# A two-layer decoder in six stages: stage boundaries reordered, weight splits halved and paced, and the second attention's order of work changed

## The reference, cut to what matters

```python
x = x + L0_attn(layernorm(x))     # stage A: latent attention
x = x + L0_xattn(layernorm(x), ctx, ctx, 0, mask)   # stage B, "second attention"
x = x + L0_ffn(layernorm(x))      # stage C: x @ W_up.T + LoRA of the expert with the largest gate
x = x + L1_attn(layernorm(x))     # stage D: gated FFN (1248) and a six-term series
x = x + L1_xattn(layernorm(x), ctx)                 # stage E: 8 "heads" of 64, 128 keys
x = x + L1_ffn(layernorm(x))      # stage F: relu(x @ up)**2 @ down and a routed latent part, then layernorm
...
# stage B, per sequence: 32 heads of 16, keys and values shared by 4 heads
scores = einsum('bgrst,..', xq, xk) / 4 + mask
out = einsum('bgrst,btgd->bsgrd', softmax(scores), xv)
# stage D
dterm = exp(log|delta| * m - discount[m-1])         # m = 1 .. 6, delta = x @ gate_w.T - local_point
out = approx_up @ approx_out.T + sum((dterm * approx_up) @ fuse[m-1].T) \
      + (silu(x @ ffn_gate_w.T) * (x @ ffn_up_w.T)) @ ffn_down_w.T
```

## Time and profile before

| what | value |
|---|---|
| median of 3 runs | 1254.52 us (1254.37 to 1260.95) |
| the profiled execution's own time | 1251.37 us |
| its span | 1249.6 us, mean granted PE clock 0.955 |
| PE busy | 1109.9 us (89%) |
| DVE busy | 738.6 us (59%) |
| ACT busy | 464.2 us (37%) |
| POOL busy | 423.4 us (34%) |

### The profile page before, as it was taken

One profiled execution on the slowest core, in us unless ns is written; L12 is line 12 of the kernel. 1 busy time (PEld: TensorE's weight loads), 2 busy tenths in 40 slices (PEclk: granted clock), 3 DMA queues, 4 the chain that ended last, 5 costly groups with the idle time before them and its releaser, 6 DMA issues.

```text
span 1249.6 us, 23652 instructions
## 1 busy us (share of the span) xinstructions
PE 1109.9 (89%) x9380; PEld 594.0 (48%) x9380; DVE 738.6 (59%) x1255; ACT 464.2 (37%) x813; POOL 423.4 (34%) x365
## 2 busy tenths in 40 slices
PE   6798886988898789998799999999888799999992
PEld 3454453666664344444344444444455444444441
DVE  6777774788887674348613511532479833646456
ACT  4566562555555534321111211211256522223220
POOL 2355495788851320039500000000043300506053
PEclk9897995899999999999999999999999999999997
DMA  6000100111110111222100000000000000000000
GB/s 231 2 3 2 29 2 27 40 41 41 39 55 24 62 42 44 99 78 76 51 1 1 0 0 0 1 1 1 3 11 7 1 1 1 26 8 34 0 34 34
DMA packets 29011, 35.91 MB, mean 29 GB/s; under 512 B 5882, under 2 KB 20499, under 8 KB 28788
## 3 DMA queue, kind: packets, MB, share of 16 engines
q1 hardware_dynamic: 27506, 34.53, 8.4%
q10 hardware_dynamic: 1410, 0.06, 0.1%
HBM read 30.24 MB, written 4.19 MB: 28 GB/s over the span
## 4 chain that ended last, share of the span: by engine, by line
PE 58%; DVE 19%; issue 3%; ACT 3%; POOL 0%; DVEq 0%; ACTq 0%; POOLq 0%
PE p_up L116 10%; PE p_up L118 9%; PE p_up L117 9%; PE p_y L116 7%; PE p_y L118 7%; PE p_y L117 7%; DVE b_top L1355 2%; DVE wf_lo L241 2%; DVE e_den L2197 1%; PE p_y L1511 1%; ACT wd_hi L2246 1%; DVE e_top L2187 1%; PE p_up L110 1%; PE p_up L1499 1%; DVE d_term L1893 1%
## 5 line engine op out<-in xcount | busy, mean ns | idle before, releaser
L1902 DVE TENSOR_TENSOR d_h_low<-d_hf,d_h_high 128x512 f16<-128x512 f32 (+1 forms) x40 | 32.0, 799 | 199.9 <-ACT d_h_high L1979 199.9
L116 PE MATMUL p_up<-d_xt_high,wd_hi 128*128 128x512 f16 (+1 forms) x352 | 133.4, 379 | 2.9 <-PE p_y L118 1.5
L117 PE MATMUL p_up<-d_xt_low,wd_hi 128*128 128x512 f16 (+1 forms) x352 | 133.4, 379 | 0.0
L118 PE MATMUL p_up<-d_xt_high,wd_lo 128*128 128x512 f16 (+1 forms) x352 | 133.4, 379 | 0.0
L129 POOL TENSOR_SCALAR ve<-mv 128x4 f32<-128x4 f32 x16 | 4.9, 306 | 340.2 <-DVE mv L188 319.2
L116 PE MATMUL p_y<-wd_hi,d_h_high 128*128 128x512 f16 (+1 forms) x272 | 103.9, 382 | 9.1 <-DVE d_h_low L1902 9.0
L117 PE MATMUL p_y<-wd_lo,d_h_high 128*128 128x512 f16 (+1 forms) x272 | 103.8, 382 | 0.0
L118 PE MATMUL p_y<-wd_hi,d_h_low 128*128 128x512 f16 (+1 forms) x272 | 103.6, 381 | 0.0
L165 ACT ACTIVATE d_sg<-p_up 128x512 f32<-128x512 f32 (+1 forms) x40 | 23.8, 594 | 210.2 <-PE p_up L118 210.2
L430 POOL TENSOR_TENSOR a_pt_low<-a_ex,a_pt_high 128x1024 f16<-128x1024 f32 x32 | 68.2, 2131 | 75.1 <-ACT a_pt_high L919 75.0
L2460 DVE TENSOR_TENSOR d_h_low<-d_hf,d_h_high 128x512 f16<-128x512 f32 x32 | 27.5, 858 | 68.2 <-ACT d_h_high L2549 68.2
(11 more groups left out here) (331 smaller groups left out, 3023.6 us busy)
## 6 DMA issues: line engine op xcount, KB each, us to landing
wd_raw<-in_w_d SPq DMA_DIRECT2D x16, 616.0 KB, 3.5
wd_raw<-in_w_f SPq DMA_DIRECT2D x8, 578.0 KB, 3.5
X<-in_x SPq DMA_DIRECT2D x4, 1024.0 KB, 12.1
wd_lo<-in_ctx_t SPq DMA_DIRECT2D x128, 32.0 KB
out_x<-wd_raw SPq DMA_DIRECT2D x16, 256.0 KB, 2.0
wd_lo<-in_ctx SPq DMA_DIRECT2D x32, 64.0 KB, 2.3
wd_raw<-in_w_c SPq DMA_DIRECT2D x1, 1096.0 KB, 12.5
wd_hi<-in_Wo SPq DMA_DIRECT2D x1, 1024.0 KB
```

The source lines that it names most:

```text
L116: nc.tensor.matmul(ps, st[0], mv[0], start=start, stop=False)
L117: nc.tensor.matmul(ps, st[0], mv[1], start=False, stop=False)
L118: return nc.tensor.matmul(ps, st[1], mv[0], start=False, stop=stop)
L1902: nc.vector.tensor_tensor(hid[1][0:n, d % NH, :], value, hid[0][0:n, d % NH, :], ALU.subtract).then_inc(h_ready, 1)
```

## The change: what it does, and its diff

1. Stage B: on PE `turn_p(n)` comes ahead of `shift(n+1)`; on ACT `high_p(n)` ahead of `expo(n+1)`; on DVE `norm_o(n-2)` and `update` come after `low_x`/`norm` and `low_p(n)`.
2. Stage C: the two ACT instructions of a weight piece are issued after two successive tiles (the rounding after t in EARLY, the scaling one tile later).
3. Stage D: POOL waits before each of the eight splits of stage F's weights for a hidden block of stage D: pieces 0 to 4 for the blocks d = 7 to 11 of chunk 1, pieces 5 to 7 for d = 7 to 9 of chunk 2.
4. Stage D to E: DVE adds the last four tiles first and measures them later, with the scores' maxima in between; POOL's last 1/sqrt for stage E moves behind the first two multiplications of probabilities, and the split of a folded weight from t = 1, 2 to t = 2, 3.
5. Stage E to F: the first two tiles of stage F are normalized inside stage E's last iterations and turned into banks 2 and 3 of p_up, which the scores of tile 14 leave first; tiles 2 and 3 go to banks 0 and 1. The transposes and values of tiles 14 and 15 move behind them, those of tile 15 behind the routing products.

```diff
@@ before, from line 142
 
+def turned(ps, i):
+
+    return ps[i // 2][:, i % 2, :] if isinstance(ps, tuple) else ps[:, i, :]
+
+
 def high(act, nc, c, i, t_ready, hi_ready, xt, ps):
...
     act.wait_ge(t_ready, TC * c + i + 3)
-    nc.scalar.activation(xt[0][:, :, 128 * i:128 * i + 128], ps[:, i, :].rearrange("p (k n) -> p k n", k=KB),
+    nc.scalar.activation(xt[0][:, :, 128 * i:128 * i + 128], turned(ps, i).rearrange("p (k n) -> p k n", k=KB),
                          ACT.Copy, scale=XS).then_inc(hi_ready, 1)
@@ before, from line 153
     v.wait_ge(hi_ready, TC * c + i + 1)
-    nc.vector.scalar_tensor_tensor(xt[1][:, :, tile], ps[:, i, :].rearrange("p (k n) -> p k n", k=KB), XS,
+    nc.vector.scalar_tensor_tensor(xt[1][:, :, tile], turned(ps, i).rearrange("p (k n) -> p k n", k=KB), XS,
                                    xt[0][:, :, tile], ALU.mult, ALU.subtract).then_inc(xt_ready, 1)
@@ before, from line 1390
                         p.c.low(v, 1)
-                    if n >= 2:
-                        norm_o(n - 2)
-                        if n % 2:
-                            update(n // 2 - 1)
                     if n >= 0 and n // 2 + 2 < NT:
@@ before, from line 1401
                         low_p(n)
+                    if n >= 2:
+                        norm_o(n - 2)
+                        if n % 2:
+                            update(n // 2 - 1)
                     if n + 2 < N:
@@ before, from line 1446
                         p.c.norm(act, (n - N + 4) // 2)
+                    if n >= 0:
+                        high_p(n)
                     if 0 <= n + 1 < N:
...
                     if n >= 0:
-                        high_p(n)
                         if n % 2 == 0 and n // 2 + 2 < NT:
@@ before, from line 1531
                 for n in range(-2, N + 1):
+                    if 0 <= n < N:
+                        turn_p(n)
                     if 0 <= n + 1 < N:
                         shift(n + 1)
-                    if 0 <= n < N:
-                        turn_p(n)
                     if n + 2 < N:
@@ before, from line 1704
             if t in EARLY:
-                weights(EARLY.index(t))
+                weights[0](EARLY.index(t))
+            if t - 1 in EARLY:
+                weights[1](EARLY.index(t - 1))
         high_next(1)
@@ before, from line 1826
                 nc.scalar.activation(held.wd_hi[:, part], raw[:, q % 2, :], ACT.Copy, scale=WS).then_inc(wd_high, 1)
+
+            def scale_first(act, q):
                 act.wait_ge(wd_high, q + 1)
@@ before, from line 1833
                     part = slice(PF * q, PF * q + PF)
+                    pool.wait_ge(h_ready, DND + G6 + 2 + q if q < 5 else 2 * DND + G6 + 2 + q - 5)
                     split_piece(nc, pool, raw[:, q % 2, 0:PF], held.wf_hi[:, part], held.wf_lo[:, part],
...
                 pool.wait_ge(wf_split, 3 * NP_F)
-                for c in range(NC):
+                for c in range(NC - 1):
                     rstd_chunk(nc, pool, held, c, stats, held.rs_e + 2 * c)
+
+            def gpsimd_last(pool):
+                rstd_chunk(nc, pool, held, NC - 1, stats, held.rs_e + 2 * NC - 2)
 
@@ before, from line 1928
                 values(NC - 1, {}, True)
+
+                def add(i):
+                    t = NT - TC + i
+                    v.wait_ge(y_ready, t + 1)
+                    nc.vector.scalar_tensor_tensor(held.X[:, t, :], p_y[:, i, :], 1.0 / (HS * WS), held.X[:, t, :],
+                                                   ALU.mult, ALU.add).then_inc(y_read, 1)
+
+                def measure(i):
+                    stats_tile(v, nc, held, NC - 1, i, y_read, NT - TC + i + 2, (held.apart, stats))
                 e.soft(v, 0)
-                update_one(NC - 1, 0)
-                update_one(NC - 1, 1)
+                add(0)
+                add(1)
+                e.soft(v, 1)
                 e.total(v, 0)
-                e.soft(v, 1)
-                update_one(NC - 1, 2)
-                update_one(NC - 1, 3)
+                add(2)
+                add(3)
+                measure(0)
                 e.total(v, 1)
+                for i in range(1, TC):
+                    measure(i)
 
@@ before, from line 1979
                             high_weights(weights[d])
-                c_part.scalar(act, lambda q: high_first(act, q),
+                c_part.scalar(act, (lambda q: high_first(act, q), lambda q: scale_first(act, q)),
                               lambda i: high(act, nc, 0, i, t_ready, hi_ready, xt, p_up))
@@ before, from line 2075
                 pe.wait_ge(y_read, NT + 1)
-            d.low_first, d.high_first = low_first, high_first
+            d.low_first, d.gpsimd_last = low_first, gpsimd_last
             d.sync, d.gpsimd, d.vector, d.scalar, d.tensor = sync, gpsimd, vector, scalar, tensor
@@ before, from line 2155
 
-    def gpsimd(pool):
+    def gpsimd(pool, last_rstd):
         for t in range(NT):
...
                 ALU.mult).then_inc(prob_ready, 1)
-            if t in (1, 2):
-                l = t - 1
+            if t == 1:
+                last_rstd(pool)
+            if t in (2, 3):
+                l = t - 2
                 pool.wait_ge(w2_copy, l + 1)
@@ before, from line 2203
 
-    def vector(v):
+    def vector(v, norm_next):
         for w in range(2, NT):
...
                 norm(v, w + 1)
+            else:
+                norm_next(0)
             if w >= 3:
...
                 total(v, w - 1)
+        norm_next(1)
         soft(v, NT - 1)
@@ before, from line 2264
         expo(act, NT - 1)
-        values(act, NT - 2)
 
@@ before, from line 2330
         output(pe, NT - 3)
-        transposes(pe, NT - 2)
     e.fetch_weights, e.clear_weights, e.fold_in, e.keys_in, e.fold, e.make_keys = \
@@ before, from line 2416
 
+            f.turned = held.p_up[:, 2:4, :], held.p_up[:, 0:2, :]
+
+            def norm_first(v, i):
+                if i == 0:
+                    v.wait_ge(held.rs_ready, held.rs_f + 2)
+                if i >= 2:
+                    v.wait_ge(t_ready, i + 1)
+                norm_tile(nc, held, xn[:, i % 2, :], i).then_inc(xn_ready, 1)
+
             def vector(v):
@@ before, from line 2481
                                                 ALU.subtract, ALU.mult).then_inc(normed, 1)
-                def norm(i):
-                    v.wait_ge(t_ready, i + 1)
-                    norm_tile(nc, held, xn[:, i % 2, :], i).then_inc(xn_ready, 1)
-
                 def low_x(i):
-                    low(v, nc, 0, i, hi_ready, xt_ready, xt, p_up)
-                v.wait_ge(held.rs_ready, held.rs_f + 2)
-                norm(0)
-                norm(1)
+                    low(v, nc, 0, i, hi_ready, xt_ready, xt, f.turned)
+                norm_first(v, 2)
+                norm_first(v, 3)
                 low_x(0)
-                norm(2)
                 low_x(1)
-                norm(3)
                 e.update(v, NT - 2)
@@ before, from line 2521
                     for i in range(TC):
-                        high(act, nc, c, i, t_ready, hi_ready, xt, p_up)
-                        if first and i == 1:
-                            e.values(act, NT - 1)
+                        high(act, nc, c, i, t_ready, hi_ready, xt, f.turned if first else p_up)
+                        if first and i % 2:
+                            e.values(act, NT - 2 + i // 2)
                     for l in range(FL):
@@ before, from line 2572
                     last.then_inc(logit_ready, 1)
+                    if first:
+                        e.transposes(pe, NT - 1)
                     for l in range(FL):
@@ before, from line 2628
                     pe.wait_ge(xn_ready, i + 1)
-                    transpose_tile(nc, held, p_up[:, i, :], xn[:, i % 2, :]).then_inc(t_ready, 1)
-                pe.wait_ge(e.exp_ready, NT)
+                    if i % 2 == 0:
+                        pe.wait_ge(e.exp_ready, NT - 1 + i // 2)
+                    transpose_tile(nc, held, turned(f.turned, i), xn[:, i % 2, :]).then_inc(t_ready, 1)
                 turn_one(0)
                 turn_one(1)
+                e.transposes(pe, NT - 2)
                 e.output(pe, NT - 2)
-                e.transposes(pe, NT - 1)
                 turn_one(2)
@@ before, from line 2641
                 blocks(NC - 1, False)
+            f.norm_first = norm_first
             f.sync, f.gpsimd, f.vector, f.scalar, f.tensor = sync, gpsimd, vector, scalar, tensor
@@ before, from line 2690
                 d.gpsimd(pool)
-                e.gpsimd(pool)
+                e.gpsimd(pool, d.gpsimd_last)
                 f.gpsimd(pool)
...
                 d.vector(v)
-                e.vector(v)
+                e.vector(v, lambda i: f.norm_first(v, i))
                 f.vector(v)
```

## The result

| | before | after |
|---|---|---|
| median of the runs | 1254.85 us (4 runs, 1254.37 to 1260.95) | 1234.21 us (4 runs, 1230.97 to 1237.96) |
| ratio after to before | | 0.9828, 95% interval 0.9803 to 0.9854 |
| profiled execution, its span | 1251.37, 1249.6 us | 1230.97, 1229.2 us |
| mean granted clock | 0.955 | 0.950 |

The changed kernel is 20.6 us faster by the medians (21.6 by the ratio); the forecast was 27.0 (1227.5, range 1219 to 1238, in which the measured time lies).

What follows compares the result with a forecast made beforehand. PE was 89% busy, so gains lie in its gaps, in stages B, C, D and E's edges. 14.7 + 6.5 + 2.4 + 1.6 + 1.8 = 27.0 us, taking 1254.5 to 1227.5; range 1219 to 1238.

Steps and rivals of the forecast that it cites:

- Stage D: Pacing POOL's splits brings chunk 1 and the way into it to clean lengths: 14.7 us won, bounds 5.2 and 15.2.
- Rivals (3): Stage D: paced pieces stall chunk 1 as before, only the way into it is clean; 1237.0 us, chance 0.10.
- (5): Stage D: the waits don't bind and POOL splits as before; 1242.2 us, chance 0.04.
- Stage C: Weight-piece halves after two successive tiles: a pair takes 9.7 instead of 10.18 us; 2.4 us won, bounds 0 and 6.
- no hold at all: Stage C's upper bound, 6 us: POOL's subtraction would not hold the next tile's gate step.
- Stage D to E: Later measurements fill DVE's idle time before the loop's first maximum: 1.6 us won, bounds 0 and 3.7.
- E to F: Normalizing stage F's first tiles ahead removes PE's 4.99 us wait: 1.8 us won, bounds 0 and 4.5.
- Stage B: New unit order: pairs 3.5, first four units 2.3, last two and way out 0.7; 6.5 us won.
- The chain of 10.1 us: Stage B, two units: shift to attend, half turn_p, high_p, two low_p, norm_o, update, maximum; 10.1 instead of 10.36 to 10.4.
- Rival (1): Stage B gains nothing, its circle closed over norm_o and attend instead of the exponential; 1234.0 us, chance 0.12.
- rival (2): Stage B runs at DVE's own pace until it meets POOL, which lets through 9.3 us; 1224.7 us, chance 0.13.
- Rival (4): Stage B: turn_p delays shift and norm_o delays attend in both units, 49 us lost there; 1283 us, chance 0.03.

Runs made afterwards that it cites:

- the pacing alone: Kernel before plus only the eight waits ahead of POOL's splits of stage F's weights: 1241.27 us, ratio 0.9886.
- Place and hold together: Changed kernel, stage C's weight halves issued ahead of high_z and POOL's subtraction held until the next tile's low part is out: 1222.42 us, ratio 0.9742.
- The experiment on these two units: Changed kernel, with norm_o ahead of low_p on VectorE in the last two units of stage B: 1229.18 us, ratio 0.9783.
- 0.9796: Changed kernel, stage C's halves ahead of high_z but POOL's subtraction not held for the next tile's low part: 1230.72 us, ratio 0.9796.

## Why the prediction was right, and where it was not

- **Stage D** (14.7): 15.1 in the traces, 14.8 by the medians of the pacing alone. Chunk 1 came to 104.3 and the way into it to 15.7, the clean lengths of the earlier trace rows within 0.3. The 0.5 for a collision left over was not needed. Rivals (3) and (5) are out: no term is slow and the waits bind.
- **Stage C** (2.4): 2.8, with the tiles at the predicted 4.46 and 5.2. The bound of 6 "no hold at all" was too small; it kept ScalarE's place and took away the hold alone. Place and hold together are worth 11.1, 12.8 without the slow first tile.
- **Stage D to E** (1.6): 1.7, the idle time before the first maximum gone. **E to F** (1.8): 2.2, as 4.9 ahead of F's first product less 2.7 behind it.
- **Stage B** (6.5) is the term that was mis-sized: its own worth is 3.2, and 1.7 without a pair of units that ran at a lower clock, though the first two traces show 6.2. Against the old order with all else changed, the five intervals at the start gave 1.7 (forecast 2.3) and the pairs behind them 2.6 (3.5, at 10.17 to 10.44 us and not 10.1 throughout), with 1.5 more from that one pair. By the forecast's own figures, 10.36 less 10.1, 15 pairs give 15 x 0.26 = 3.9 and not 3.5. The failed step is "the last two units and the way into stage C give 0.7": they lose 2.7, 0.8 in the last interval and 1.9 after it. The text had named the mechanism (norm_o, which attend waits for, stands behind low_p) and gave it no price at the end, where no maximum hides it. The experiment on these two units shows it for the part after the last maximum, where it wins back 2.35; the last interval stays 5.63 us in it, and its 0.8 is not separated.
- The chain of 10.1 us was added up with VectorE's order taken as given. It holds low_p's wait, norm_o and update in series; the rival price, the same sum with them ahead of low_p, was not worked out. The experiments give the shares: PE's and ACT's moves together win 7.0 us, VectorE's gives 3.7 to 3.9 of them back. PE's and ACT's moves were not run one by one.
- Rival (1), "the circle is closed over norm_o", and rival (2), "the stage meets POOL", each describe in part what runs show: in the changed kernel norm_o stands in the circle of the maxima, though attend does not (norm_o has no idle time ahead of it in the pair above), and the kernel with VectorE's old order meets POOL. Rival (4) is out: no pair of the changed kernel is over 10.44 us.
- **The clock.** The miss in the first traces is 6.3 us in stage A and 1.5 between C and D; both vary without the change too (204.9 to 209.8 and 7.6 to 9.3 over the three traces with the old stages A to C). The forecast started from one execution of before whose stage A was short, and treated unchanged code as unchanged time. Against 17 runs of before beside 6 of the changed kernel the gain is 25.4 us by the medians (23.7 by the ratio); with the first four runs each it is 20.6 (21.6). The edits' own worths add up to 3.2 + 2.8 + 15.1 + 1.7 + 2.2 = 25.0: four terms came out 0.1 to 0.4 above the forecast and stage B's 3.3 below it.

## What to carry to other kernels

Where a long GpSimd instruction holds VectorE, try to place it: give it a wait for the moment after which VectorE's two-input work is done. That won 15 us in stage D and, by the ratios 0.9796 and 0.9742, about 7 of the 9 in stage C; shortening the instruction was not tried. When a reorder moves the same step on several engines, price each engine's move by itself: here two of them gained 7.0 us together and the third took over half of it back. And before a sum is made, compare the stages that the change doesn't touch over more than one execution.

## What the runs showed of the hardware

- The same code of stage A took 204.8 to 211.2 us over 14 traces, with the mean granted clock of 80 to 200 us between 0.81 and 0.86; the spread is 0.5% of the kernel's time.
- The hold also catches a short instruction: a 128x32 one went from 0.18 to 2.28 us. The Trainium skill, "SBUF — State Buffer", section "Who interferes with whom", says that the pair is locked for a whole instruction; the trace agrees, 2.28 of POOL's 2.52 us.
- Stretches of lower clock come in stage B in either order, and their time and depth differ. With VectorE's old order PE was busy 19.97 of 20 us in 250 to 270, and in 290 to 310 the granted clock was 0.84, part of the stretch at 1.2 GHz instead of 2.4; in the changed kernel, with PE busy 18.55, it was 1.00 there. But all four traces of the old order have 0.83 in 330 to 340, with PE busy 17.7 to 18.5 of the 20 us before, and three of the nine traces with the new order on all three engines (two of them altered in the last two units) have 0.66 to 0.70 there. So a denser stage as the cause is not shown.
